# Adjacency tiles loaded as bf16 through GpSimd's DMA queue, in a sparse graph-attention layer

## The reference

```
q = x @ Wq.T + bq;  k = key @ Wk.T + bk;  v = value @ Wv.T + bv
s = (q @ k.T) / 64 * adj
s = where(|s| < 1e-5, -1e9, s)
out = layernorm(x + (softmax(s) @ v) @ Wm.T + bm)
```

## Time and profile before

| | |
|---|---|
| median of 3 runs | 562.37 us (561.5 to 562.74) |
| profiled execution | 560.05 us, its span 558.2 us |
| busy in the span | PE 510.8, DVE 337.4, ACT 229.7, POOL 232.0 us |
| mean granted clock of TensorE | 0.973 |
| moved by DMA | 160.81 MB, mean 288 GB/s |

### The profile page before, as it was taken

How to read it: one execution, slowest core, us unless ns; L and a number is a source line. 1 busy time by engine, 2 the same in 40 slices (tenths; PEclk the granted TensorE clock), 3 DMA queues, 4 the chain that set the end, 5 groups by cost and what they waited for, 6 DMA issues and landing times.

```text
span 558.2 us, 5679 instructions
## 1 busy us (share of the span) xinstructions
PE 510.8 (92%) x1678; PEld 267.3 (48%) x1678; DVE 337.4 (60%) x756; ACT 229.7 (41%) x463; POOL 232.0 (42%) x205
## 2 busy tenths in 40 slices
PE   6999999999389974999999989999999999999983
PEld 3444444444134443556555545555555555555651
DVE  1574678976961047678688888765645543453552
ACT  0233123333123222334552554464373464465473
POOL 3000020008600366466675565655664565466400
PEclk9999999999879996999999999999999999999996
DMA  9999999999999999595899899656547455346422
GB/s 350 423 406 426 426 422 387 384 397 418 408 395 356 340 418 389 175 360 206 320 383 408 318 292 354 217 162 212 164 150 242 105 182 187 99 144 227 114 76 79
DMA packets 43957, 160.81 MB, mean 288 GB/s; under 512 B 9874, under 2 KB 9874, under 8 KB 37778
## 3 DMA queue, kind: packets, MB, share of 16 engines
q1 hardware_dynamic: 20690, 102.21, 47.0%
q0 software_dynamic: 16992, 38.26, 22.3%
q10 hardware_dynamic: 6240, 19.92, 9.0%
HBM read 161.98 MB, written 25.17 MB: 335 GB/s over the span
## 4 chain that ended last, share of the span: by engine, by line
PE 43%; DMA 22%; DVE 19%; SPq 8%; ACT 4%; issue 3%; POOL 0%; ACTq 0%; DVEq 0%; POOLq 0%
DMA big<-adj_tiles 16%; PE bank L496 13%; PE bank L602 11%; PE bank L622 10%; SPq L353 7%; DVE big L898 7%; PE bank L578 5%; DMA table<-key 4%; DMA kv<-table,index 2%; PE bank L612 1%; DVE big L933 1%; DVE slots L931 1%; PE bank L593 1%; DVE big L901 1%; DVE score L1035 1%
## 5 line engine op out<-in xcount | busy, mean ns | idle before, releaser
L392 POOL DMA_INDIRECT kv<-table,index x90 | 100.1, 1112 | 111.5 <-PE bank L622 89.2
L487 PE MATMUL bank<-kv,big 128*128 128x512 f32 x256 | 113.6, 604 | 10.6 <-DMA big<-valueT 10.6
L496 PE MATMUL bank<-big,M 128*128 128x512 f32 x256 | 120.0, 596 | 0.0
L421 POOL DMA_INDIRECT adj_g<-adj_cols,index x96 | 107.8, 1123 | 29.3 <-issue 29.3
L898 DVE TENSOR_TENSOR big<-big 128x2048 bf16<-128x2048 f32 x32 | 73.2, 2288 | 41.3 <-DMA big<-adj_tiles 41.3
L602 PE MATMUL bank<-keyT,qT 128*128 128x384 f32 x256 | 88.9, 490 | 6.2 <-issue 4.9
L622 PE MATMUL bank<-kv,probT 128*128 128x512 f32 x192 | 89.7, 604 | 0.9 <-ACT probT L809 0.6
L487 PEld LDWEIGHTS bank<-kv,big 128*128 128x128 f32 x256 | 49.1, 193 | 72.6 <-issue 61.0
L602 PEld LDWEIGHTS bank<-keyT,qT 128*128 128x128 f32 x256 | 47.6, 190 | 46.7 <-issue 19.1
L496 PEld LDWEIGHTS bank<-big,M 128*128 128x128 f32 x256 | 44.6, 192 | 34.2 <-issue 34.2
L1030 DVE SCALAR_TENSOR_TENSOR score<-bank,c_cols,adjT 128x384 f32<-128x384 f32 x32 | 19.8, 618 | 67.8 <-PE bank L602 66.4
(11 more groups left out here) (99 smaller groups left out, 522.4 us busy)
## 6 DMA issues: line engine op xcount, KB each, us to landing
big<-adj_tiles SPq DMA_DIRECT2D x32, 2048.0 KB, 11.3
big<-valueT ACTq DMA_DIRECT2D x8, 1024.0 KB, 13.4
x_buf<-x SPq DMA_DIRECT2D x32, 256.0 KB, 4.5
table<-key SPq DMA_DIRECT2D x8, 1024.0 KB, 22.8
out<-y_buf SPq DMA_DIRECT2D x32, 256.0 KB, 3.7
big<-xT SPq DMA_DIRECT2D x6, 1024.0 KB, 12.0
table<-qT ACTq DMA_DIRECT2D x4, 1024.0 KB, 20.9
table<-y_buf ACTq DMA_DIRECT2D x4, 1024.0 KB, 28.5
```

Source lines behind the costliest of these rows:

```text
L392: pool.indirect_dma_start(kv[:, b, c, :], None, table, bass.IndirectOffsetOnAxis(index[:, t, c:c + 1], 0), bounds_check=N - 1, oob_is_err= ...
L421: pool.indirect_dma_start(adj_g[:, b, c, :], None, adj_cols, bass.IndirectOffsetOnAxis(index[:, t, CH + c:CH + c + 1], 0),).then_inc(adj_g ...
L487: mm = nc.tensor.matmul(bank[4 + t % 2][:, :], col_buf[nb % 2][:, d, k * P:(k + 1) * P], G[:, d, :], start=(d == 0), stop=(d == DC - 1))
L496: mm = nc.tensor.matmul(ps[:, :], M[:, d, a * P:(a + 1) * P], col_buf[nb % 2][:, d, :], start=(d == 0), stop=(d == DC - 1))
```

## The change

Each adjacency tile now arrives as bf16 (the DMA converts on the way), in four buffers of 8 KiB per partition in the same 32 KiB of `big`. Transfers that convert are started by GpSimd, so all `load_adj` leave SP's program and stand in POOL's, at places written out by hand: 0 to 3, then POOL's first memset, 4 to 11, a wait for the weights' products and the second memset, 12 to 18, then the early gathers, 19, 20 and 21, then the gathers of values, and in the main loop one load behind each tile's gathers, two iterations ahead of its tree. The first step of the tree reads bf16 in place of float32. SP's program keeps the other loads, the copies of `key` and the stores.

```diff
+AB = 4
-        adj_buf = [big[:, i * 4096:(i + 1) * 4096] for i in range(2)]
+        adj_buf = [big[:, i * 2048:(i + 1) * 2048].bitcast(BF16) for i in range(AB)]
-        adj_in = [sem(f"adj_in{i}") for i in range(2)]
+        adj_in = [sem(f"adj_in{i}") for i in range(AB)]
 # SP
-            def load_adj(t):
-                if t >= 2:
-                    sp.wait_ge(adj_used, t - 1)
-                sp.dma_start(adj_buf[t % 2], adj_tiles[t]).then_inc(adj_in[t % 2], 16)
-            for t in range(4):
-                load_adj(t)
-            for t in range(4, FIRST):
-                load_adj(t)
-            for t in trees_of(0):
-                load_adj(t)
-                for t in trees_of(i + 1):
-                    load_adj(t)
 # POOL
+            def load_adj(t):
+                if t >= AB:
+                    pool.wait_ge(adj_used, t - AB + 1)
+                pool.dma_start(adj_buf[t % AB], adj_tiles[t]).then_inc(adj_in[t % AB], 16)
+            for t in range(AB):
+                load_adj(t)
             nc.gpsimd.memset(kv_flat[:, 0:kv_half], 0.0).then_inc(kv_zeroed, 1)
+            for t in range(AB, 3 * AB):
+                load_adj(t)
             pool.wait_ge(prep_ps, 2 * DC + 3)
             nc.gpsimd.memset(kv_flat[:, kv_half + 2048:2 * kv_half], 0.0).then_inc(kv_zeroed, 1)
+            for t in range(3 * AB, FIRST - 1):
+                load_adj(t)
             pool.wait_ge(index_ready, 2 * CH)
 ...
             for t in range(EARLY, KV):
                 gather_adj(t)
+            load_adj(FIRST - 1)
+            for i in range(2):
+                for t in trees_of(i):
+                    load_adj(t)
             pool.wait_ge(spare_sb, KV)
 ...
-            for t in range(EARLY, T):
-                gather(t)
+            gather(EARLY)
+            for i in range(T - KV + 1):
+                gather(i + KV - 1)
+                for t in trees_of(i + 2):
+                    load_adj(t)
 # DVE, reduce_tile
-                dve.wait_ge(adj_in[t % 2], 16 * (t // 2 + 1))
+                dve.wait_ge(adj_in[t % AB], 16 * (t // AB + 1))
-                nc.vector.tensor_tensor(t1, adj_buf[t % 2][:, 0:2048], adj_buf[t % 2][:, 2048:4096], ALU.logical_or
+                nc.vector.tensor_tensor(t1, adj_buf[t % AB][:, 0:2048], adj_buf[t % AB][:, 2048:4096], ALU.logical_or
```

## The result

The changed kernel takes 574.76 us (median of 4 runs, 572.41 to 576.6), the kernel before 561.93 us (4 runs, 559.07 to 562.74). The ratio is 1.0235, 95% interval 1.0182 to 1.0289: slower by 13 us, where 11 us faster was forecast. The profiled execution took 574.22 us, its span is 572.4 us.

A forecast was written before the change was run, and what follows sets the result against it. It took full DMA engines, with PE close behind, to bound the opening, and PE or DVE the loop. 560.05 us minus 6 (opening) minus 5 (loop) is 549; 2.3 for median over profiled execution makes 551.3, range 535 to 590.

The forecast's parts named there:

- these 18.9 us: PE's two long stalls in the opening, 10.60 us for the last `valueT` and 8.32 for the gather of tile 2.
- The transfer itself: Adjacency tiles: a converting transfer paced by bytes read, 4.9 us per tile; 2.45 if written bytes set the pace.
- The rivals of a cheaper and a dearer tile: Tile transfers: cheaper at 2.45 us, total 537, chance 0.18; dearer, above 4.9 us, total 563 to 602, chance 0.23.
- The first step of the tree: DVE's L898 on bf16: 1.06 us gained per tree, hidden in the opening, 5 us in the loop over five iterations.
- Loads on POOL: POOL in the loop: 1.3 us per load, which fits, or nearly, in its slack; nothing shows in the opening.
- the rival in which POOL becomes the bound: In the loop, 4.3 us per load against 3.3 us of slack at 12.1 us; total 571, chance 0.08.
- Moving the loads off SP: Opening: queues take turns by packet; copies of `key` get about a ninth of the rate, tiles slow by some 12%.
- The end of the opening: Start of `keys(2)`: about 210.5 us, a gain of 6, with -5 and 9 as bounds.
- The count of bytes at full engines: Opening: all that `keys(2)` needs was moved by 216.7 us; the floor with tiles at 4.9 us is about 210.5.
- The chain behind the last store: Before `keys(2)`: POOL's wait for the stores ends at 188.7, then gathers, memset and landing; `keys(2)` at 207.
- the 18.5 us of the prediction: POOL before `keys(2)`: at least this for six gathers of values, a memset, three gathers and a landing, against 28 before.
- What would show it: Signs to check, among them L898 at 1.2 us, `keys(2)` near 211 us, iterations of 11.0 us; slower: stalls at `lists` or `spread_slots`.

The follow-up runs named there:

- weights_first: The changed kernel, but POOL starts tile 0 only when the constants, wq and wk have landed: 568.76 us, ratio 1.0146.
- one_queue: The changed kernel with two tiles in flight, wq and wk issued by POOL behind tile 3, the copies of `key` behind tile 18: 571.21 us, ratio 1.0158.
- two_in_flight: The changed kernel with four buffers, but each load waits for the tree two tiles back, so only two tiles are queued: 556.32 us, ratio 0.99.
- hold_two: The changed kernel, but tiles 2 and 3 wait on POOL for the constants, then four are in flight: 564.05 us, ratio 1.0014.
- late_key: The changed kernel, but x and the eight copies of `key` are held on SP until 16 trees are done: 565.61 us, ratio 1.0086.
- quarter_rows: The changed kernel, but each tile comes as four transfers of a quarter of the columns, in rows of 4 KiB: 567.2 us, ratio 1.0102.
- hold_two_late_key: The changed kernel, but tiles 2 and 3 wait for the constants, and x and the copies of `key` for tree 16: 551.75 us, ratio 0.9843.

## Why the prediction was wrong

*What bounds the opening.* "Nothing in the opening can give back more than these 18.9 us" bounded the gain; nothing bounded the loss. PE's other inputs, the constants and the weights, were taken to arrive as before.

*The transfer itself: right.* 4.9 us was taken, 5.2 measured, for converting and plain tiles alike. By the Trainium skill, page "DMA: Bandwidth & Descriptors", section "Where 436 GB/s comes from", the ports on the side of SBUF are the bottleneck, which would give half: no run here agrees with that for a converting load (292.6 us of the engines with float32 written, 291.4 with bf16). The same section adds that between HBM and SBUF the side of HBM binds; the unchanged time agrees with that, though the figure given there, about 358 GB/s, is below the 428 of the earlier trace rows. The rivals of a cheaper and a dearer tile are both out.

*The first step of the tree: right, with some luck in the sum.* 1.07 us per tree; 5.3 us in the loop where 5 was taken. But not as five iterations of 12.1 us that give 1.06 each. From keys(8) to keys(13) the five steps were 11.62, 10.95, 12.10, 12.12 and 13.69 us, which average 12.1; they became 11.62, 10.56, 10.56, 10.56 and 11.89. Three gave 1.5 to 1.8 us, as those of 12.1 fell to 10.56 and not to 11.0, one gave 0.4 and one nothing.

*Loads on POOL: right that they fit, mis-sized.* 0.58 us, not 1.3; the rival in which POOL becomes the bound is out. (POOL's work of an iteration was also taken as 8.4 us there; the earlier trace rows give 8.7.)

*Moving the loads off SP: the step that failed.* It found the law (equal turns by packet), and applied it to the copies of `key`, the stores and the tiles only. It said of wq, wk, x and the copies that "their work only changes place". Three things were overlooked; their prices overlap and don't add up. First, wq, wk and the constants had been in the tiles' own queue or ahead of it, and were served in order; now each of their packets of 0.10 us waits for one of 0.56 us. weights_first shows it by taking the tiles away, and one_queue agrees. The law was in the text and the sum could have been done: 32 turns per engine for the 512 rows of a 1 MiB weight, at 0.56 + 0.1 + 0.1 us, make 24 us (an estimate from the packets of 5 to 27 us), and wq and wk landed 23.7 and 24.4 us after the transfer ahead of them. Second, the four buffers, which the prediction gave no price: with two in flight POOL's queue ran empty while DVE waited for the constants, and the weights passed; with four it had packets at every turn up to some 85 us (two_in_flight and hold_two against the changed kernel: 18.4 and 10.7 us by the medians). Third, the copies of `key` now take turns beside the tiles through most of the opening (late_key, 9 us).

*The end of the opening: failed with it.* The count of bytes at full engines assumes that they stay full. They were at 0.41 and 0.51 from 196 to 224 us. 6 us gained were forecast for the start of keys(2), 21.6 us were lost. The chain behind the last store, the other bound of the prediction, moved too: POOL's wait for the stores ended at 213.0 us, where it had ended at 188.7. With the 18.5 us of the prediction that gives 231.5, and PE came to keys(2) at 238.3: the chain didn't bind, but only because PE was late itself.

*What would show it.* The signs named for a slower kernel were stalls at `lists` or `spread_slots`. There were none over 0.9 us in the changed kernel (quarter_rows has one of 34); they were at the constants, at wk and at `valueT`. And `table<-key` was to be issued before 10 us: SP came to it at 43.8, held by four small loads (last section).

In sum, for the two profiled executions: 560.05 plus 21.6 up to keys(2), minus 2.2 for the low clock that no longer follows the stall before keys(2), minus 5.3 in the ten iterations behind keys(3), is 574.2, and 574.22 was measured.

Left open: what the place of tiles 12 to 18 behind the products costs, and how the 6.9 us that the conversion saves in the opening at depth two divide between shorter trees and earlier buffers.

## What to carry to other kernels

When a transfer changes its queue, list everything that was served in order with it and is now served beside it: DMA engines here give each queue with work one packet in turn, so a queue of large rows takes most of the time (0.56 us of an engine against 0.10 at each turn) and one of small rows is slow beside it: 1 MiB of a weight took some 24 us once its turn in its own queue had come, 47 and 71 us from issue, and 7 to 13 us inside the tiles' queue. A full set of DMA engines is a bound only if the order in which it works is the order in which the rest needs the data; price the first inputs of the critical engine before the total. More buffers can be more pressure on the other queues: a wait that looks like lost time (two buffers, late constants) may be what lets the urgent transfers through, and hold_two_late_key, which keeps the conversion and puts two such waits in, is 1.6% faster than the kernel before.

## What the runs showed of the hardware that was not expected

- A converting transfer of 2 MiB float32 to bf16 costs the DMA engines what the plain one costs, 5.2 us, although half the bytes are written.
- Four times smaller rows of the same bytes (4 KiB read, quarter_rows) cost 0.7 us more per 2 MiB tile.
- A direct load of 128 rows takes POOL 0.58 us, a gather of 128 rows about 1.0.
- SP itself is held when its queue is slow. In the changed kernel four small loads of x, with no wait in the program, took SP from 4.80 to 43.8 us to issue; issued at 124 us in hold_two_late_key they took 1.81 us (start, us, issue):

```profile
4.80 38.96 SPq L330 DMA_DIRECT2D x_buf<-x  x4
43.80 80.07 SPq L345 DMA_DIRECT2D table<-key  x8
```
